# A two-layer transformer kernel: k projection as one product, one full-height causal mask, and modulation rows broadcast by TensorE

## The reference, cut to what matters

```python
mod = (_silu(L0_c) @ L0_wmod).reshape(8, 6, 1, -1)
sa, ca, ga, sb, cb, gb = (mod[:, i] for i in range(6))
ga = (2 * (ga >= 0) - 1) * jnp.maximum(jnp.abs(ga), 0.25)   # gb likewise
h = _layernorm(x) * (1 + ca) + sa
latent = h @ Wc_down
q = (latent @ Wq_up).reshape(8, 512, 16, 8)
kv = latent @ Wkv_up
k, v = kv[..., :8], kv[..., 8:]                  # one k and v for all 16 heads
att = einsum('bthd,bsd->bhts', q, k) / sqrt(8)
att = softmax(where(causal, att, -inf))
y = einsum('bhts,bsd->bthd', att, v).reshape(8, 512, 128)
x = x + ga * (y @ Wc_proj)
h = _layernorm(x) * (1 + cb) + sb
x = x + gb * moe_ffn(h)        # 8 experts of 1024 tokens; then layer 1
```

## Time and profile before

| | us |
|---|---|
| median of 3 runs (1092.03 to 1093.64) | 1093.1 |
| the profiled execution, its own time | 1092.03 |
| its span, first to last instruction | 1090.3 |
| TensorE busy in the span | 784.8 |
| VectorE busy in the span | 596.4 |
| GpSimd busy in the span | 487.5 |
| ScalarE busy in the span | 436.8 |

### The profile page before, as it was taken

How to read it: one execution, slowest core, us unless ns; L and a number is a source line. 1 busy time by engine, 2 the same in 40 slices (tenths; PEclk the granted TensorE clock), 3 DMA queues, 4 the chain that set the end, 5 groups by cost and what they waited for, 6 DMA issues and landing times. The chain is left out here.

```text
span 1090.3 us, 16627 instructions
## 1 busy us (share of the span) xinstructions
PE 784.8 (72%) x6063; PEld 414.0 (38%) x6063; DVE 596.4 (55%) x1399; ACT 436.8 (40%) x691; POOL 487.5 (45%) x573
## 2 busy tenths in 40 slices
PE   4277999989999999725224688667606699999884
PEld 2132333333333333224112456445403355555543
DVE  4376766867666674115673333331114488888761
ACT  1002554545454455501002222222235577777661
POOL 6121010513313132343007788888746567775423
PEclk9566999999899998955556888888855799999996
DMA  4202344253331411210001222223320110110100
GB/s 111 62 4 65 77 118 97 56 154 86 57 87 41 98 52 31 71 50 1 0 0 42 36 38 39 37 40 43 32 36 11 24 27 21 31 31 21 27 15 19
DMA packets 69430, 51.44 MB, mean 47 GB/s; under 512 B 20256, under 2 KB 63272, under 8 KB 68776
## 3 DMA queue, kind: packets, MB, share of 16 engines
q1 hardware_dynamic: 58088, 41.75, 15.3%
q0 software_dynamic: 11264, 8.66, 6.0%
HBM read 31.30 MB, written 16.99 MB: 44 GB/s over the span
## 5 line engine op out<-in xcount | busy, mean ns | idle before, releaser
L625 DVE TENSOR_REDUCE MX<-bank 128x1 f32<-128x512 f32 (+3 forms) x352 | 215.6, 639 | 97.9 <-PE bank L386 93.9
L495 ACT ACTIVATE PR<-ps_s 128x1024 f32<-128x1024 f32 x160 | 159.0, 1023 | 150.9 <-PE ps_s L350 86.1
L383 PE MATMUL bank<-K,Q 96*128 96x512 bf16 (+3 forms) x512 | 134.4, 322 | 39.8 <-DMA Q<-d_q 19.4
L1029 POOL DMA_INDIRECT d_acc<-Y,idx x64 | 107.7, 1683 | 22.9 <-issue 18.9
L1019 POOL DMA_INDIRECT XG<-d_tab,idx x64 | 77.8, 1215 | 80.7 <-DVE idx L1139 62.1
L383 PEld LDWEIGHTS bank<-K,Q 96*128 96x128 bf16 x512 | 44.4, 102 | 159.2 <-DVE MX L625 113.3
L341 PE MATMUL ps_s<-Q,K 99*128 99x512 bf16 x320 | 96.7, 390 | 1.3 <-DMA Q<-d_m 1.3
L386 PE MATMUL bank<-maskT,identb 128*128 128x128 bf16 (+2 forms) x352 | 91.3, 259 | 0.0
L366 PE MATMUL bank<-PR,VE 128*32 128x512 f32 x640 | 89.3, 631 | 0.2 <-ACT PR L495 0.2
L703 POOL TENSOR_SCALAR ve<-mv 128x4 f32<-128x4 f32 x8 | 1.9, 234 | 186.8 <-DVE mv L568 186.8
L1283 ACT ACTIVATE H<-ps_h,b1T 128x512 f32<-128x512 f32 x64 | 43.9, 687 | 92.9 <-PE ps_h L1233 62.3
(11 more groups left out here) (275 smaller groups left out, 1419.5 us busy)
## 6 DMA issues: line engine op xcount, KB each, us to landing
Q<-d_q SPq DMA_DIRECT2D x24, 384.0 KB
d_q<-qs SPq DMA_DIRECT2D x24, 128.0 KB, 2.3
d_y<-ysb SPq DMA_DIRECT2D x128, 18.0 KB
d_tab<-tab SPq DMA_DIRECT2D x8, 272.0 KB, 2.4
X<-L_attn_x SPq DMA_DIRECT2D x8, 256.0 KB, 4.9
w<-L_ffn_W SPq DMA_DIRECT2D x8, 256.0 KB, 3.5
d_acc<-zrow SPq DMA_DIRECT2D x1, 2048.0 KB, 9.2
yt<-d_y SPq DMA_DIRECT2D x8, 256.0 KB, 3.3
```

The costliest lines, as they stand in the source:

```text
L383: nc.tensor.matmul(ps_mx[G % 2][:, x * w:(x + 1) * w], Q[b % QB][0:KR, h, P * g:P * g + P], K[b % QB][0:KR, 0:w], start=(x == 0), stop=Fal ...
L495: nc.scalar.activation(PR[t % 2][:, 2 * half:2 * half + 2, :], ps_s[half][:, :].rearrange("p (a f) -> p a f", a=2), ACT.Exp, scale=DH ** - ...
L625: nc.vector.tensor_reduce(MX[b % 2][:, c:c + len(hs)], ps_mx[G % 2][:, 0:len(hs) * w].rearrange("p (x w) -> p x w", w=w), AX_X, ALU.max).t ...
L1029: nc.gpsimd.indirect_dma_start(out=g.d_acc, out_offset=bass.IndirectOffsetOnAxis(ap=idx[:, e, k:k + 1], axis=0), in_=Y[e % 2][:, k, :], in ...
```

## The change

Three edits, all in the attention stage.

1. `k` is one product of 512 columns with 8 outputs. Its parts have the shape [8, 512] where they had [128, 128], and one DMA stores them.
2. The mask of a diagonal step is two products of 128 rows by 512 columns (`maskT` against the broadcast identity) where there were four of 64 by 256. `maskX` and its four GpSimd instructions in the set-up go.
3. The modulation rows no longer pass through DRAM. A new use `bc` of `ps_misc` in step 1 of batch n-1 multiplies the rows (`modR`) with a one-hot matrix, which puts the batch's 384 values in all partitions. ScalarE copies scale and shift to SBUF (`cbsb`), VectorE makes `wg` straight from PSUM.

```diff
-MISC0 = {2: [("hT", 2)], 3: [("k", 2)], ...
+MISC0 = {1: [("bc", -1)], 2: [("hT", 2)], 3: [("k", 2)], ...
-    ks = sb0("ks", [P, PARTS, P], BF16)
-    kr = sb0("kr", [P, P])
+    ks = sb0("ks", [DH, PARTS, T], BF16)
+    kr = sb0("kr", [DH, T])
@@ PE, scores_T
             if i == g:
-                for c in range(2):
-                    part = ps_s[half][:, 512 * c:512 * c + 512].rearrange("p (h q) -> p h q", q=P)
-                    eye = bc(identb[64 * c:64 * c + 64, 64 * c:64 * c + 64].unsqueeze(1), [64, 4, 64])
-                    for turn in range(2):
-                        o = 64 * (c ^ turn)
-                        last = nc.tensor.matmul(part[:, :, o:o + 64], (maskT, maskX)[turn][64 * c:64 * c + 64, :], eye,
-                                                start=False, stop=(turn == 1), tile_position=(64 * c, 0),
-                                                skip_group_check=True)
+                for hh in range(2):
+                    last = nc.tensor.matmul(ps_s[half][:, 512 * hh:512 * hh + 512], maskT[:, :],
+                                            bc(identb[:, :].unsqueeze(1), [P, 4, P]), start=False, stop=True)
@@ PE, misc
             elif kind == "k":
-                for i in range(NT):
-                    last = nc.tensor.matmul(m[32 * i:32 * i + DH, 0:P], w_fold[:, D:D + DH], hT[:, P * i:P * i + P],
-                                            start=True, stop=True, tile_position=(0, 32 * i))
+                last = nc.tensor.matmul(m[0:DH, :], w_fold[:, D:D + DH], hT[:, :], start=True, stop=True)
+            elif kind == "bc":
+                pe.wait_ge(s_modR, 2)
+                last = nc.tensor.matmul(m[:, 0:384], onehot[:, b, :], modR[:, 0, 2 * D:5 * D], start=True, stop=True)
             elif kind == "pj":
-                pe.wait_ge(S["wg_rdy"], b + 1)
@@ ACT, misc
-                nc.scalar.activation(ks[:, 0, :], m[:, 0:P], ACT.Copy).then_inc(S["k1_rdy"], 1)
+                nc.scalar.activation(ks[:, 0, :], m[0:DH, :], ACT.Copy).then_inc(S["k1_rdy"], 1)
+            elif kind == "bc":
+                full((kind, b))
+                if b >= 2:
+                    act.wait_ge(S["h2_rdy"], b - 1)
+                nc.scalar.activation(cbsb[b % 2][:, :, :], m[:, D:3 * D].rearrange("p (a d) -> p a d", a=2),
+                                     ACT.Copy).then_inc(S["cb_rdy"], 1)
@@ DVE
-                nc.vector.tensor_tensor(kr[:, :], m[:, 0:P], ks[:, 0, :], ALU.subtract).then_inc(S["misc_free"], 1)
+                nc.vector.tensor_tensor(kr[:, :], m[0:DH, :], ks[:, 0, :], ALU.subtract).then_inc(S["misc_free"], 1)
+            elif kind == "bc":
+                dve.wait_ge(S["cb_rdy"], b + 1)
+                nc.vector.tensor_tensor(wg[:, :], m[:, 0:D], w_cp[:, :], ALU.mult).then_inc(S["misc_free"], 1)
-                if 0 <= b < NB and s == 1:
-                    dve.wait_ge(DS[f"cb_in{b % 2}"], 16 * (b // 2 + 1))
-                    nc.vector.tensor_tensor(wg[:, :], cb[b % 2][:, 0, :], w_cp[:, :], ALU.mult).then_inc(S["wg_rdy"], 1)
@@ SP
-                if n == -1 and s == 3:
-                    sp.wait_ge(s_modR, 2)
-                    sp.dma_start(d_cb, modR[:, 0, 2 * D:5 * D]).then_inc(DS["cb_st"], 16)
-                    sp.dma_start(cb[n % 2][:, :, :].rearrange("p a d -> p (a d)"),
-                                 bass.AP(d_cb.tensor, 3 * D * n, [[0, P], [1, 3 * D]])).then_inc(DS[f"cb_in{n % 2}"], 16)
-                    for i in range(NT):
-                        sp.dma_start(bass.AP(d_k[par].tensor, P * i, [[T, DH], [DH * T, PARTS], [1, P]]),
-                                     ks[32 * i:32 * i + DH, :, :]).then_inc(DS[f"k_st{par}"], 16)
+                    sp.dma_start(bass.AP(d_k[par].tensor, 0, [[T, DH], [DH * T, PARTS], [1, T]]),
+                                 ks[:, :, :]).then_inc(DS[f"k_st{par}"], 16)
```

More of the change, by code:

```diff
@@ L108, in full @@
         return self.index[u] // self.banks + 1
-MISC0 = {2: [("hT", 2)], 3: [("k", 2)], 4: [("q", 2)], 5: [("v", 2)], 6: [("h2", -2)],
+MISC0 = {1: [("bc", -1)], 2: [("hT", 2)], 3: [("k", 2)], 4: [("q", 2)], 5: [("v", 2)], 6: [("h2", -2)],
          7: [("m", 1), ("lg", -2)], 8: [("pj", -1)]}
@@ L193, in program @@
     b1T = sbm("b1T", [P, NE, NC_DI])
-    maskX = sb0("maskX", [P, P], BF16)
     cT = sb0("cT", [P, 2, NB])
@@ L231, in program @@
     wg = sb0("wg", [P, D])
-    cb = [sb0(f"cb{i}", [P, 3, D]) for i in range(2)]
+    cbsb = [sb0(f"cbsb{i}", [P, 2, D]) for i in range(2)]
     stat2 = sb0("stat2", [P, NT, 6])
@@ L257, in program @@
              "mv_rdy", "rs_rdy", "xn_rdy", "q1_rdy", "q2_rdy", "q3_rdy", "k1_rdy", "k2_rdy", "k3_rdy",
-             "m_rdy", "y_ev", "rc_rdy", "yn_rdy", "wg_rdy", "mv2_rdy", "rs2_rdy", "xn2_rdy", "h2_rdy", "lgx_rdy", "tab_rdy"]
+             "m_rdy", "y_ev", "rc_rdy", "yn_rdy", "cb_rdy", "mv2_rdy", "rs2_rdy", "xn2_rdy", "h2_rdy", "lgx_rdy", "tab_rdy"]
     S = {n: sem("a0_" + n) for n in names}
     dnames = ["q_st0", "q_st1", "k_st0", "k_st1", "q_in0", "q_in1", "m_st", "m_in0", "m_in1", "y_st0", "y_st1",
-              "yt_in", "lc_in", "r_st", "rl_in", "tab_st", "cb_st", "cb_in0", "cb_in1"]
+              "yt_in", "lc_in", "r_st", "rl_in", "tab_st"]
     DS = {n: sem("a0_" + n) for n in dnames}
@@ L342, in scores_T @@
                                         Q[b % QB][0:KM, 4 * hg:4 * hg + 4, P * g:P * g + P],
-                                        start=True, stop=(i < g), skip_group_check=(i == g))
+                                        start=True, stop=(i < g))
             if i == g:
-                for c in range(2):
-                    part = ps_s[half][:, 512 * c:512 * c + 512].rearrange("p (h q) -> p h q", q=P)
-                    eye = bc(identb[64 * c:64 * c + 64, 64 * c:64 * c + 64].unsqueeze(1), [64, 4, 64])
-                    for turn in range(2):
-                        o = 64 * (c ^ turn)
-                        last = nc.tensor.matmul(part[:, :, o:o + 64], (maskT, maskX)[turn][64 * c:64 * c + 64, :], eye,
-                                                start=False, stop=(turn == 1), tile_position=(64 * c, 0),
-                                                skip_group_check=True)
+                for hh in range(2):
+                    last = nc.tensor.matmul(ps_s[half][:, 512 * hh:512 * hh + 512], maskT[:, :],
+                                            bc(identb[:, :].unsqueeze(1), [P, 4, P]), start=False, stop=True)
             last.then_inc(S["sT_full"], 1)
@@ L473, in misc @@
                 if b >= 1:
-                    act.wait_ge(DS[f"k_st{(b - 1) % 2}"], 64 * ((b - 1) // 2 + 1))
-                nc.scalar.activation(ks[:, 0, :], m[:, 0:P], ACT.Copy).then_inc(S["k1_rdy"], 1)
+                    act.wait_ge(DS[f"k_st{(b - 1) % 2}"], 16 * ((b - 1) // 2 + 1))
+                nc.scalar.activation(ks[:, 0, :], m[0:DH, :], ACT.Copy).then_inc(S["k1_rdy"], 1)
[5 more added lines that the diff above has]
+                                     ACT.Copy).then_inc(S["cb_rdy"], 1)
             elif kind == "h2":
@@ L679, in _ @@
                                    pattern=[[-1, P]], channel_multiplier=1))
[L680 to L683, removed]
         lk(nc.gpsimd.memset(onehot[:, :, :], 0.0))
@@ L728, in _ @@
                     pool.wait_ge(S["xn2_rdy"], b + 1)
-                    pool.wait_ge(DS[f"cb_in{b % 2}"], 16 * (b // 2 + 1))
+                    pool.wait_ge(S["cb_rdy"], b + 1)
                     if b >= 1:
@@ L733, in _ @@
                     h = tab[:, :, 0:D]
-                    lk(nc.gpsimd.tensor_tensor(h, xn2[:, :, :], bc(cb[b % 2][:, 2:3, :], [P, NT, D]), ALU.mult))
-                    nc.gpsimd.tensor_tensor(h, h, bc(cb[b % 2][:, 1:2, :], [P, NT, D]),
+                    lk(nc.gpsimd.tensor_tensor(h, xn2[:, :, :], bc(cbsb[b % 2][:, 1:2, :], [P, NT, D]), ALU.mult))
+                    nc.gpsimd.tensor_tensor(h, h, bc(cbsb[b % 2][:, 0:1, :], [P, NT, D]),
                                             ALU.add).then_inc(S["h2_rdy"], 1)
```

8 lines of the change are left out of this document (1 added, 7 removed).

## The result

The forecast was slower, 1104.0 us (1097 to 1110). The change is slower: median 1104.36 us of 4 runs (1101.35 to 1106.47) against 1092.57 of 4 (1087.70 to 1093.64) of the kernel before, ratio 1.0114, 95% interval 1.0072 to 1.0157. Measured again with more runs (experiment 10) the ratio was 1.0148, 1.011 to 1.0187. The profiled execution took 1103.56 us, span 1101.8; before it was 1092.03 and 1090.3.

The account below looks back on a forecast made before the run. TensorE was taken to bound the kernel, VectorE second where TensorE waits for it; 6.8 + 1.9 + 0.8 + 1.2 + 1.0 = 11.7 us on 1092.03 gave 1103.7, put at 1104.0 for the higher median; range 1097 to 1110.

Parts of the forecast that it names:

- k on TensorE, +0.48: k projection in the attention loop: the single product takes 0.97 us where the old took 0.49, 0.48 more.
- k on VectorE, +0.65: k projection: kr goes from 0.23 to 0.68 us and the cast from 0.23 to 0.43, +0.65 together.
- In series: k projection: TensorE's 0.48 and VectorE's 0.65 us add up to 1.13 per round, with ScalarE's copy hidden.
- Nothing gives the 1.13 back: Loop rounds 0 to 5: no later TensorE wait for VectorE absorbs k's delay, so 6 x 1.13 = 6.8 us.
- Growth of a round, 1.2 to 1.3 with both edits: Attention loop: rounds with both bc and k get 1.2 to 1.3 us longer, rounds with k only 1.1.
- the sign that was set: Attention rounds: forecast wrong if they grow by only about 0.5 us, by over 1.9, or their clock differs from before.
- Round -1, +1.9: Round ahead of the loop, at lower clock: k product 1.26 us more plus VectorE's 0.65, making 1.9.
- Round -2, +0.8: Earliest round: k's third part 1.4 us later, one store for four saves up to 0.8; net +0.8, between 0.3 and 1.6.
- bc, 0.09 per batch: Modulation product behind the first maxima pair: two waits swallow 0.60 us, leaving 0.09; round 7 pays 0.7; sum 1.2.
- The mask, +0.01 per half: Causal mask of the scores: 0.87 us per half against 0.86, 64 times 0.6, plus 0.4 at low clock; together 1.0.
- Set-up, 0: Start-up: removing the GpSimd instructions for maskX, ahead of a barrier that others reach later, changes nothing: 0 us.
- the prediction's third rival: Whole attention loop: the clock falls more often, three more such rounds, +10 us, 1114; chance 0.06.

Follow-up runs that it names:

- experiment 10: The changed kernel with all three edits, measured once more in more runs beside the kernel before: 1105.60 us, ratio 1.0148.
- experiment 8: The changed kernel with k weights zero-padded to 128 outputs, one-hot and modulation rows to 128 rows: 1097.85 us, ratio 1.0069 to the kernel before.
- Experiment 5: The kernel before with k as one product of 512 columns on TensorE, other engines and stores unchanged, later keys left out: 1096.13 us, ratio 1.0056.
- Experiment 6: The kernel before with one extra VectorE clear of 620 elements behind the cast of k: 1095.17 us, ratio 1.0042.
- Experiment 1: The kernel before with the k edit alone (one product, [8, 512] parts, one store): 1101.13 us, ratio 1.0111.
- Experiment 3: The kernel before with only the modulation rows broadcast by TensorE, k and mask as before: 1096.37 us, ratio 1.0065.
- experiment 9: The kernel before with the query-buffer clears moved (Q[0] first, Q[1] and Q[2] later), the mask edit, and no maskX set-up: 1082.95 us, ratio 0.9936.

## Why the prediction was right, point by point

The direction and the main mechanism were right: k costs on TensorE and on VectorE in series. The total is right in part by luck. Against the rows, the terms 6.8, 1.9, 0.8, 1.2, 1.0 and 0 came out as 7.2, 1.1, 0.6, 2.8, 0.6 and -1.5; the errors cancel to 0.9. Two things that the sum did not have, waits for loads and the clock's loss, pull in opposite directions.

- **k on TensorE, +0.48.** Measured 0.62. The streaming was right (experiment 8: 0.91); the delay of 0.15 ahead of it was taken to go with the four column tiles, and it stays with one product of 8 outputs.
- **k on VectorE, +0.65.** The rows give `kr` +0.39 and the cast +0.18, so 0.57. On 8 partitions `kr` takes 0.62 where 128 took 0.68. The errors cancel: 1.13 was predicted, 1.20 measured.
- **In series.** Right, by experiments 5 and 6. The wait behind the scores, 0.67 before, is 1.24 (about 1.3 forecast). ScalarE's copy was hidden (it ends at 363.20, `kr` starts at 363.87).
- **"Nothing gives the 1.13 back", six rounds.** Right from round 2 on. In rounds 0 and 1 the waits for loads of Q gave back about 1.9 us of k and bc together. The earlier trace rows had such a wait, and it was read only for what stands ahead of the loop.
- **Growth of a round, 1.2 to 1.3 with both edits.** 1.6 at equal clock (48.29 to 49.91). By the sign that was set, over 1.9 or another clock, the forecast would have failed in the third round (48.29 at 0.96, then 51.52 at 0.93): a round can only be compared with one at the same clock.
- **Round -1, +1.9.** Measured 1.1. The k product at low clock took 2.04 with what stands ahead of it (1.97 forecast), 0.79 before, so 1.25 more, as forecast (1.26). But the q product behind it, 1.82 before, now ran at full clock, 0.91, which no term foresaw. The rows of TensorE, before and then after:

```profile
74.61 2.02 PE L397 MATMUL bank<-hT,w_fold 128*128 128x512 f32 x2
76.43 0.63 PE L383 MATMUL bank<-K,Q 96*128 96x512 bf16 x1
```
```profile
69.82 1.88 PE L393 MATMUL bank<-hT,w_fold 128*8 128x512 f32 x2
71.62 0.50 PE L376 MATMUL bank<-K,Q 96*128 96x384 bf16 x1
...
75.14 1.08 PE L390 MATMUL bank<-hT,w_fold 128*128 128x512 f32 x2
76.05 0.38 PE L376 MATMUL bank<-K,Q 96*128 96x512 bf16 x1
```

- **Round -2, +0.8.** Measured 0.6: the third part came later, one store (0.34 of issue) took the place of four (1.54).
- **bc, 0.09 per batch.** Measured 0.33. The mechanism (the two waits swallow 0.60, round 7 pays in full) was right; the product was mis-sized, 0.99 for 0.75, by what its 8 rows cost (experiment 8). Of the two waits, only one names VectorE in the earlier trace rows.
- **The mask, +0.01 per half.** Right to the hundredth; its 0.4 for blocks at low clock was not separable.
- **Set-up, 0.** Wrong by 1.5 us. "Ahead of a barrier that others reach later" looked at who reaches the barrier and not at what the clear behind it holds up. The row was there to be read: 7.12 us for an instruction whose like takes 0.27.
- **The sum.** 11.7 predicted, 10.8 by the local rows, some 9 less what the loads give back, +11.5 between the two spans. The medians moved by 11.8 (1104.36 - 1092.57) and 17.0 (1105.60 - 1088.65). With 11.7 on its median of 1093.1 the forecast would have been 1104.8; the text added 0.3 to 1103.7.

Open: the median grows by more than the local rows add in most kernels where work was added. Changed kernel: 10.8 by rows, 11.8 and 17.0 measured. Experiment 1: 8.9 and 10.5. Experiment 3: 2.8 and 5.7. Experiment 5: 6 x 0.62 = 3.7 and 6.6. Experiment 6: 6 x 0.60 = 3.6 and 5.7. Experiment 8, though: 10.8 - 6 x 0.15 - 6 x 0.24 - 0.09 = 8.4, and 8.4 measured. The clocks of the single runs bear on it. Span times (1 - granted clock) is what a run lost against full clock. It averages 184.5, 185.8 and 185.3 us in the three sets of the kernel before (60 runs, one run scatters by some 3), 190.0 in the 5 runs of the result, 189.8 in experiment 10, 188.0 in 1, 188.5 in 3 and 188.2 in 6, but 184.2 in 8. So where the median grew by more than the rows, the clock as a rule lost 2.4 to 4.5 us more, and in experiment 8 it did not. Experiment 5 does not fit (185.4), and experiment 8 has nearly the work of the changed kernel. That added work makes the clock fall more often, the prediction's third rival, is therefore not shown; none of the runs held the clock fixed.

## What to carry over

Before an edit on the critical path is priced, ask of each engine on the chain whether its part is in series: put the same time there by itself, one engine at a time, as in experiments 5 and 6; if the halves add up, so will the edit. Then compare whole rounds at equal granted clock, for a wait elsewhere in the round, here for loads, can give the price back. Look in the start-up for an instruction that lasts many times its like, and at what the neighbouring engine does when it ends: moving three clears was worth 6.5 us in the profile, and 7.2 between the medians, as much as the 7.2 that the rows give for k in the loop. A product with few rows or few outputs is to be priced with what it costs on both sides, or padded.

## What was not expected of the hardware

Two instructions of VectorE that read and write SBUF (`sT_e`, `gtmp`) are held until GpSimd's clear ends, one of them through two clears back to back (7.12 us for 0.27), while a copy from PSUM is not (0.19), nor are VectorE's own clears (0.48 in experiment 9 beside the clear of Q[0], and 0.48 in the kernel before, where that clear comes later). In the profile the held time looks like work of VectorE and names no releaser. A product with 8 outputs, or with 8 rows, pays 0.15 ahead of it instead of 0.06, as the explicit tiles do, and 0.05 (k) and 0.14 (bc) more until the next one. The Trainium skill, "TensorEngine Tiling (Array Packing)", section Key Properties, ties the drain to a change of tiling mode. The runs show the same 0.15 for a product that asks for no tile, and that it goes with padding; that it is that drain is likely and not shown.
